# A spectral conv stack in NCHW: the forward transform over w as two 64-row matmul tiles

## The reference

```
x = x + conv3x3(gn(x))                 # 32 -> 32 channels
x = x + column_scan(gn(x))             # a gated recurrence over the 64 columns w
x = x + irfft2(low modes of rfft2(gn(x)) * complex weights, 16 x 16 modes)
x = x + irfft2(rfft2(gn(x)) * complex weights, all 64 x 33 modes) + bias
```

## Time and profile before

| what | value |
|---|---|
| median of 3 runs | 608.94 us (608.06 to 610.95) |
| the profiled execution | 607.1 us, of which the span on the core is 605.3 us |
| PE busy | 550.9 us, 91% |
| PEld busy | 459.3 us, 76% |
| DVE busy | 472.8 us, 78% |
| ACT busy | 402.6 us, 67% |
| POOL busy | 300.5 us, 50% |

### The profile page before, as it was taken

The page is one execution under the profiler, slowest core; times in us unless marked ns, Lnnn a source line. Parts: engine busy times, 40 slices in busy tenths (PEclk is TensorE's granted clock), DMA queues, the critical chain, the costliest instruction groups (busy, mean ns, idle before and its releaser), DMA issues.

```text
span 605.3 us, 21551 instructions
## 1 busy us (share of the span) xinstructions
PE 550.9 (91%) x7884; PEld 459.3 (76%) x7884; DVE 472.8 (78%) x1272; ACT 402.6 (67%) x897; POOL 300.5 (50%) x425
## 2 busy tenths in 40 slices
PE   3699999799999999999999999988789887999996
PEld 2233333489899999899999999988577676899995
DVE  7569896567777777777777778799989999577876
ACT  2344969866666666666667977885557977766441
POOL 7456655045565555565655122024789799321100
PEclk9799999989999999999999999999999999999999
DMA  6900000011111111111111300000327766103324
GB/s 226 378 2 0 2 2 5 0 42 36 43 39 39 43 35 43 39 39 42 36 43 27 140 2 1 0 1 19 123 92 232 230 215 202 41 1 140 139 122 157
DMA packets 21282, 45.66 MB, mean 75 GB/s; under 512 B 5104, under 2 KB 15600, under 8 KB 20352
## 3 DMA queue, kind: packets, MB, share of 16 engines
q1 hardware_dynamic: 20160, 44.97, 23.1%
q10 hardware_dynamic: 672, 0.15, 0.1%
q0 software_dynamic: 416, 0.07, 0.1%
HBM read 28.53 MB, written 8.39 MB: 61 GB/s over the span
## 4 chain that ended last, share of the span: by engine, by line
PE 38%; DVE 32%; ACT 15%; issue 9%; POOL 3%; DVEq 2%; DMA 1%; POOLq 0%; SPq 0%; ACTq 0%
PE psum L645 8%; DVE work L326 5%; PE psum L756 5%; PE psum L895 5%; PE psum L911 5%; DVE spec L1344 5%; ACT spec L1002 5%; DVE spec L1336 5%; ACT spec L1010 5%; DVE spec L1339 4%; PE psum L772 4%; DVE small L1222 3%; PE psum L814 3%; PE psum L884 2%; PE psum L740 2%
## 5 line engine op out<-in xcount | busy, mean ns | idle before, releaser
L685 PE MATMUL psum<-spec,matrices 128*64 128x128 f32 x2016 | 154.0, 274 | 1.6 <-issue 1.5
L681 PE MATMUL psum<-spec,matrices 128*64 128x128 f32 x1512 | 132.4, 282 | 6.2 <-DVE spec L1344 3.7
L685 PEld LDWEIGHTS psum<-spec,matrices 128*64 128x64 f32 x2016 | 119.3, 138 | 2.5 <-issue 1.7
L522 POOL TENSOR_TENSOR spec<-spec 32x120 f32<-32x120 f32 x126 | 59.7, 474 | 87.1 <-DVE spec L1339 87.1
L681 PEld LDWEIGHTS psum<-spec,matrices 128*64 128x64 f32 x1512 | 85.1, 137 | 20.2 <-DVE spec L1344 8.5
L645 PE MATMUL psum<-spec,matrices 128*64 128x512 f32 x384 | 88.1, 616 | 9.3 <-ACT spec L936 6.3
L814 PE MATMUL psum<-work 128*32 128x128 f32 x2368 | 73.0, 274 | 15.4 <-ACT work L338 10.9
L814 PEld LDWEIGHTS psum<-work 128*32 128x32 f32 x2368 | 63.2, 110 | 25.1 <-issue 22.8
L326 DVE TENSOR_TENSOR work<-spec,psum 32x512 f32<-32x512 f32 x108 | 73.5, 680 | 3.8 <-PE psum L814 0.5
L497 POOL TENSOR_SCALAR spec<-image,small 32x960 f32<-32x960 f32 (+1 forms) x48 | 55.5, 1157 | 40.9 <-PE psum L645 21.8
L645 PEld LDWEIGHTS psum<-spec,matrices 128*64 128x64 f32 x384 | 28.0, 141 | 62.3 <-issue 53.7
(11 more groups left out here) (153 smaller groups left out, 942.5 us busy)
## 6 DMA issues: line engine op xcount, KB each, us to landing
work<-w_dram SPq DMA_DIRECT2D x33, 512.0 KB, 3.9
spec<-work SPq DMA_DIRECT2D x124, 64.0 KB, 1.9
image<-x_dram SPq DMA_DIRECT2D x3, 2048.0 KB, 11.7
out_dram<-image SPq DMA_DIRECT2D x3, 2048.0 KB, 6.3
image<-x_dram SPq DMA_DIRECT2D x4, 512.0 KB, 5.7
work<-w_dram SPq DMA_DIRECT2D x1, 2048.0 KB, 7.7
out_dram<-image SPq DMA_DIRECT2D x4, 512.0 KB, 2.9
kept<-const_dram SPq DMA_DIRECT2D x1, 192.0 KB, 6.0
```

The costliest lines, as they stand in the source:

```text
L522: nc.gpsimd.tensor_tensor(lower_edge(h, parity), below(mix[h]), below(keep[h]), ALU.subtract).then_inc(lower_ready[h], 1)
L681: mm(psum[o, 4 * h + g, 0:HB], sv[:, g, o], state[h], start=True, stop=False)
L685: last = mm(psum[o, 4 * h + g, 0:HB], sv[:, 3 + g, o], e, start=starts, stop=True)
```

## The change

`over_w` no longer issues one 128-row matmul a channel, but two of 64 rows, one for each image of the pair: the stationary operand is 64x128 (partitions 0 to 63 or 64 to 127 of `by_w`), the moving operand is that image's own 64x68 block of `fw`, without the zeros of the other image. The result goes to the same places as before. Each step is issued in two halves. The first, `straight`, alternates image 0 of channel c with image 1 of channel c + 3, whose bank is the next one; the second, `crossed`, image 1 of c with image 0 of c + 3. `crossed(k - 1)` is issued after `straight(k)` and waits for the new semaphore `w_half`, which `straight(k - 1)` raised. `w_done` is raised at the end of `crossed`. The last step has the channels 30 and 31 alone, in one bank, and so no partner. `to_spectrum` walks frequency, part, image in place of image, part, frequency: it writes four neighbouring values at a time and reads values 512 bytes apart in PSUM.

```diff
+        w_half = sem("w_half")
...
-                src = psum[:, n, :].rearrange("p (b r k) -> p b r k", b=GB, r=2)
-                dst = spec[:, :].rearrange("p (g k t r b) -> p g t b r k", g=2, k=H, t=4, r=2)
-                dst = dst[:, g, t, ds(j * GB, GB)]
+                src = psum[:, n, :].rearrange("p (b r k) -> p k r b", b=GB, r=2)
+                dst = spec[:, :].rearrange("p (g k t r b) -> p g t k r b", g=2, k=H, t=4, r=2)
+                dst = dst[:, g, t, :, :, ds(j * GB, GB)]
...
+            fw = cm["fw"].rearrange("p (r b k) -> p b r k", r=2, b=2)
+
             def over_w(j, first):
 
-                pe.wait_ge(t_act, j * 6 + 6)
-                pe.wait_ge(t_dve, j * 2 + 2)
-                for k in range(6):
+                def one_image(b, c):
+                    rows_ = slice(W * b, W * b + W)
+                    to = psum[:, (c // 3 + 4) % 8, 4 * PADK * (c % 3):4 * PADK * (c % 3) + 4 * PADK] \
+                        .rearrange("p (r b k) -> p b r k", r=2, b=2)
+                    return mm(to[:, b], bw[rows_, :, c // 2, c % 2], fw[rows_, b], start=True, stop=True)
+
+                def straight(k):
                     if not first and k < 3:
                         pe.wait_ge(h_act, j * 6 + (k - 2))
                         if k < 2:
...
                     if k >= 4:
                         pe.wait_ge(w_act, j * 12 + 2 * (k - 3))
                         pe.wait_ge(w_dve, j * 12 + 2 * (k - 3))
-                    for c in range(6 * k, min(6 * k + 6, C)):
-                        last = mm(psum[:, (c // 3 + 4) % 8, 4 * PADK * (c % 3):4 * PADK * (c % 3) + 4 * PADK],
-                                  bw[:, :, c // 2, c % 2], cm["fw"],
-                                  start=True, stop=True)
+                    for c in range(6 * k, min(6 * k + 3, C)):
+                        last = one_image(0, c)
+                        if c + 3 < C:
+                            last = one_image(1, c + 3)
+                    last.then_inc(w_half, 1)
+
+                def crossed(k):
+                    pe.wait_ge(w_half, j * 6 + (k + 1))
+                    for c in range(6 * k, min(6 * k + 3, C)):
+                        last = one_image(1, c)
+                        if c + 3 < C:
+                            last = one_image(0, c + 3)
                     last.then_inc(w_done, 1)
+
+                pe.wait_ge(t_act, j * 6 + 6)
+                pe.wait_ge(t_dve, j * 2 + 2)
+                straight(0)
+                for k in range(1, 6):
+                    straight(k)
+                    crossed(k - 1)
+                crossed(5)
```

## The result

| what | before | after |
|---|---|---|
| median, first comparison (6 runs each) | 608.5 us | 612.98 us (609.89 to 617.37) |
| ratio, 95% interval | | 1.0076 [1.0049, 1.0103] |
| the profiled execution, its span | 607.1, 605.3 us | 612.3, 610.5 us |

The account below looks back on a forecast made before the run. PE at full clock was taken to bound groups 0 to 2, and PE then DVE the last. Terms 1.2 + 0.6 + 0 - 0.9 = +0.9 us took the median from 608.94 to 609.8 us, no change; range 600 to 616.

Parts of the forecast that it names:

- turn rival: Over w: each of 10 turns between `straight` and `crossed` costs one step, +4.6 us, about 614; chance 0.13.
- The matmuls: Over w: load sets the pace, row tiles overlap, 68 steps take 7.6 to 8.0 us a group; +1.2 us.
- Switching the array: From over w to the transposes: new tiling switch of 0.20 us in groups 0 to 2; +0.6 us.
- The waits: `crossed`, `w_done` and bank 7 waits in over w: no stall, copies start 0.7 us later; 0 (0 to 0.6).
- The spectrum copy: Last group's three DVE copies: about 0.72 us each, 1.9 us instead of 2.83 on the chain; -0.9 us.
- the serial one: Over w: row tiles' loads run one behind the other, +27 to +30 us, about 637; chance 0.20.
- fast rival: Over w: a 64-row load takes half, a pair costs 59 ns, copies then bound it; about 601 us; chance 0.19.

Follow-up runs that it names:

- e7: Kernel before, each over-w matmul issued as two full-height ones of 68 columns, no row tiles: 639.24 us, ratio 1.0465; second set 643.06 us, 1.05.
- e4: Changed kernel, each one-image matmul split into two 64x64 tiles, TensorE's loop over groups 1 and 2 written out: 605.34 us, ratio 0.9928 to the kernel before.
- e2: Kernel before with only the new `to_spectrum` order: 608.51 us, ratio 0.998.
- e1: Changed kernel plus eight 128x128 identity matmuls filling TensorE's gap before over h in the last group: 613.57 us, ratio 1.0055 to the kernel before.
- e5: Four 64x64 tiles with written-out loop, plus twelve identity matmuls in the last group's gap: 603.96 us, ratio 0.9919 to the kernel before.

## Why the prediction was right or wrong

The direction that it gave the most chance, no change beyond 0.5%, did not come in the first comparison (+0.8%) and did in the second (+0.2%, or +0.4% by the plain means). That the range held 612.98 us is partly luck: its upper part stood for the turn rival and for terms of tiles and waits, and what filled it was the clock, to which the prediction gave nothing. By its own steps:

1. *The matmuls* (+1.2 forecast). The reason was right: the load of 128 columns sets the pace, row tiles overlap, a pair takes 0.118 us, and halving the columns streamed gives nothing. e7 shows it at full height, e4 from the other side. The term was mis-sized: the eight single passes of channels 30 and 31 were to cost 0.1 to 0.5 us a group, and over w takes 7.81 us as before. 128 passes took 64 paces, so they too went side by side with others: in the trace the last 20 or so loads of over w in group 0 start about 60 ns apart, one by one.
2. *Switching the array* (+0.6). The first load of the transposes comes 346.99 - (339.25 + 7.67 - 0.19) = 0.26 us after the last load of over w, 0.14 more than the pace, three times: 0.4. The three cycles together grew by 0.3 us, so nothing but this term is left in them.
3. *The waits* (0). No wait for `w_half` and none for a spectrum copy shows, and the copies start 2.4 us into over w, all as said. But the step failed in the last group, where it named nothing: the copies end 400.51 + 7.47 - 398.11 = 9.87 us after over w's start, before 9.30, since the crossed half of each step comes late. The prediction had the 0.7 us of the later start taken up by the time in which the copies were starved; only 0.13 us was, 7.47 for 7.60 us from the first copy to the last. That is the 0.57 us by which TensorE's gap grew.
4. *The spectrum copy* (-0.9). 692 and 597 ns, and 2.00 for 2.83 us on the chain: -0.8, shown by e2. That reads 512 bytes apart in PSUM would cost nothing was taken from the nearest row, and holds.

Without the clock the sum is 0.3 from the cycles and 20.31 - 20.46 = -0.15 from the last group, +0.2 us, where the prediction had +0.9. The failed step is its first sentence on bounds: "so no term below is a clock term". Full clock in the profile of before is a fact about the work before, and the change halves the columns of each pass and lengthens the gap. The term left out is what the runs measured: some 6 us in the executions where the clock falls inside over w, 1.5 to 2.7 where it falls in the last gap.

Of the rivals, the serial one fell to the 0.118 us a pair, and e7, which is that rival built (128 passes one behind the other), shows its price was right: over w takes 7.5 us more a group, and the four executions at a mean clock of 0.988 or 0.989 take 637.1 to 639.6 us, against the 637 forecast. The turn rival fell with the 7.81 us. The fast rival's condition, that a 64-row load takes half, is not met; its time, about 601, is nearly what four tiles with half the load columns get (603.96, with the loop written out).

The Trainium skill (TensorEngine Tiling (Array Packing), "Key Properties") has different tiles load and multiply in parallel, and says that a change of tiling mode drains the array: this case agrees with the first, at 0.118 us a pair; at the change a load comes 0.14 us late, which fits the second, though the draining itself stands in no row. Its page TensorE: Matmul & The Clock Gate, "LDWEIGHTS (loading the stationary operand)", has a load's time go by columns and not rows: 64x128 at 0.118 us a pair and 64x64 at 66 ns for four agree.

Open is what decides between an execution with a loss and one without. All profiles that show one in over w show it in group 0, from 340 or 341 us on (two of two), where the transposes and a wait of 0.76 us for ScalarE come before, as they do in the kernel before. In the other versions the place of a deep loss is argued from these two, since no execution of theirs with one was profiled; e7's at 0.968 were not the profiled ones. Whether over h or the transposes add to it wasn't tried apart.

## What to carry to other kernels

Before splitting a matmul into tiles, find out whether its pace is set by the columns loaded or by the columns streamed, by comparing two matmuls of different moving width: only halving the side that sets the pace gains, and here that was the load (64x64 tiles: 18.2 us a group for 19.6, 0.5 us of it perhaps the loop's). Cutting the other side gained nothing here, and the versions that did it lost clock deeply in 20 of 52 executions, so compare the granted clock of many executions and not one profile's. A copy out of PSUM that has to be strided on one side is cheaper strided in PSUM than in SBUF (0.69 for 1.04 us on VectorE, here with runs of four values written to SBUF).

## What the runs showed of the hardware that was not expected

- The clock can fall to half with TensorE busy without a break: 13 us at 0.50 with 13.00 us busy, in over w with 68 moving columns for 128 loaded ones. Twenty of 52 executions of such versions had a mean clock of 0.980 or less; of 119 with 136 columns none had. With 68 moving and 64 loaded columns (e4, e5) it was one of 15.
- The pace that the load sets follows the clock as well: of the 64 pairs in e1's 11.87 us some 22 ran in the first 2.6 us at full clock, and the other 42 in 9.3 us, 0.22 us each, against 0.118.
- An idle stretch of 2.2 us before over h is followed by half clock in some executions and not in others (over h 9.30 to 10.52 us, or 7.78). Behind over w with 136 columns and 1.7 us of idling the profiles show none; behind e7's over w with 68 columns 1.17 us were enough in one profile (9.31 us), and 1.18 us in the other cost nothing (7.78 us).
- Loads of four 64x64 tiles overlap fully: 17 ns a pass.
